# A split matmul's operands: the last chunk's low part made by two DMAs, twelve native chunks a tile instead of 38

## The chip, the cores and the metric

The kernel runs on one core of one Trainium2 chip. The metric is the device time of one execution in microseconds (us), lower is better. Engines are named as in the profile: PE is TensorE (its matmuls), PEld its weight loads, DVE is VectorE, ACT is ScalarE, POOL is GpSimd, SP is SyncE, which here only issues DMAs. A name with a q behind it (SPq, POOLq) is the queue in which that engine issues.

## The reference

A batch of 1024 samples looks up 33 rows of 128 numbers, one in each of 33 tables. From each sample's 33 rows the 528 products of all pairs are formed, sent through a small dense layer, scored against the sample's feature vector and averaged with a softmax over the pairs. A three-layer network ends it.

```python
row, col = np.triu_indices(33, k=1)
inner = x[:, row] * x[:, col]                                   # 1024 x 528 x 128
fm = relu(einsum('bpd,ad->bpa', inner, attn_W) + attn_b)        # the large matmul
scores = einsum('ba,bpa->bp', gnn_feature, fm)
attn = softmax(scores, axis=1)
attn_output = einsum('bp,bpd->bd', attn, inner) * 100.0
h = concatenate([gnn_feature, attn_output, gnn_feature], axis=1)
h = relu(h @ W_top1 + b_top1); h = relu(h @ W_top2 + b_top2); y = h @ W_top3
```

All of it is in 32-bit floating point.

## The kernel before, in words

The batch is cut into 8 tiles of 128 samples, a tile into 32 steps of 4 samples; S counts the 256 steps of the kernel, s those of a tile. One step has 4 x 528 = 2112 columns (pairs of samples and field pairs), cut into five chunks of 416 or 424 columns; two chunks fill one slot of the ring of output banks.

**One step** passes through the engines so. DVE forms the products of the pairs, 128 x 2112, into `inner` (`product`, L413). The dense layer then can be done in two ways, chunk by chunk. A **native** chunk is one matmul in 32-bit (L577), which the profile shows as two instructions. A **split** chunk takes three matmuls on operands of the type fp32r: ACT rounds the products to it (`round_inner`, L310, into `inner_hi`), DVE subtracts the rounded part from the products (`rest_of_inner`, L420, into `inner_lo`), and PE adds up low weights times high part, high weights times low part, and high times high (L584, L585, L586). The list `NATIVE` says how many chunks at the front of each step are native: one in most steps, two in six steps of a tile, four and three in the very first two. So a tile has 38 native chunks of its 160. The rounding and the subtraction run over the rest of the step in one instruction each.

ACT takes two chunks at a time out of the output banks (`relu`, L302, into `fm`). Five such pairs of chunks make up two steps; j = 0 and 1 come in the even step, 2 to 4 in the odd one. After each even step but the first PE multiplies the `fm` of the two steps before it with blocks of the feature vectors (`reduce_steps`, L607), which gives the scores.

**Beside the steps** other work of the neighbouring tiles is placed at fixed steps s by lists: at 7, 10, 13 and 16 PE multiplies the softmax weights of the tile before with its looked-up rows (`fields`, L631), and DVE weighs and sums the result one step later (L470, L478). At 18, 20, 22, 24 and 26 PE turns the looked-up rows of the next tile (`transpose_x`, L617), and ACT copies them out (L341) and repeats some of them (L331). At 19, 21 and 23 the final network of the tile before runs (`mlp`, L641 to L656; ACT L349 to L355). At the start of a tile come the row maximum (DVE L434), the exponentials (ACT L317), their scaling (ACT L326) and a transposition (DVE L450). All units that need an output bank share a ring of three banks in a fixed order.

**Queues.** Each engine's program is written out by hand in the order of the steps. In the iteration S, ACT does the first relu of S, the rounding of S + 2, then the other relus; DVE does the low part of S + 1, the weighing, and the product of S + 3. POOL only gathers: 33 indirect DMAs a tile (`gather`, L274), one after another, as soon as the rows of the tile before were turned. SP stores a tile's rows in DRAM (`store_rows`, L224), loads them again with fields and samples exchanged (`load_fields`, L213), and spreads the transposed softmax weights (`spread_attn`, L218); its order goes by tiles, with a wait ahead of each item.

**Buffers.** `inner` and `inner_hi` have three buffers, `inner_lo` two, `fm` three. The product of S waits for the low part and the native chunks of S - 3, the rounding of S for all chunks of S - 3, the low part of S for all chunks of S - 2. PE waits for a step's low part at its first split chunk.

Of the kernel before, what the change touches and what calls it, by code (L numbers as in the profile page):

```python
# [7 lines left out]
ALU = mybir.AluOpType  # L8
# [4 lines left out]
def afm_tower(nc, gnn, ids, tables, w1, b1, w2, b2, w3, attn_w, attn_b, out):  # L13
# [47 lines left out]
    LAST_FIELDS_AT = (ALL - 3, ALL - 2)  # L61

# [22 lines left out]
    with ctx:  # L85
# [12 lines left out]
        inner = sb("inner", [D, INNER_BUFS, COLS])  # L98
        inner_hi = sb("inner_hi", [D, HI_BUFS, SPLIT], FP32R)
        inner_lo = sb("inner_lo", [D, LO_BUFS, SPLIT], FP32R)  # L100
# [11 lines left out]
        w3_sb = sb("w3_sb", [P, M2])  # L112
        b1_sb = sb("b1_sb", [P, M1])
        b2_sb = sb("b2_sb", [P, M2])
        attn_wt = sb("attn_wt", [D, P])
        attn_wt_hi = sb("attn_wt_hi", [D, P], FP32R)
        attn_wt_lo = sb("attn_wt_lo", [D, P], FP32R)
        attn_b_sb = sb("attn_b_sb", [P, 1])
        gnn_t = sb("gnn_t", [P, B])
        pooled = sb("pooled", [D, P])  # L120
        h1 = sb("h1", [P, M1, P])
        h2 = sb("h2", [P, M2, P])
        y_row = sb("y_row", [1, P])
        ident = sb("ident", [P, P])
        neg_max = sb("neg_max", [P, 1])
        exp_sum = sb("exp_sum", [P, 1])
        inv_sum = sb("inv_sum", [P, 1])


        gnn_rows = x_fields[:, 0, 0:T, :]  # L130
        attn_w_rows = x_fields[:, 1, 0, :]
        weighted = attn[:].rearrange("p a b -> p (a b)").rearrange("p (b f) -> p b f", f=I)
        weighted_tail = inner[:, 0, 0:QS * FN * I].rearrange("p (b f) -> p b f", f=I)
# [20 lines left out]
        s_lo = sem("inner_lo_ready")  # L154
        s_hidden = sem("hidden_ready")
# [39 lines left out]

        def native_cols(S):
            return EDGES[S % 2][NATIVE[S]]

# [9 lines left out]
        def _(sp):  # L208
# [11 lines left out]

            def store_rows(t):
# [15 lines left out]
            store_rows(1)  # L237
# [4 lines left out]
            for t in range(T - 1):  # L242
                sp.wait_ge(s_inv, 3 * (t + 1))
                spread_attn(0)
                spread_attn(1)
                for c in (2, 3):
                    sp.wait_ge(s_fields_done, FJ * t + c - 1)
                    load_fields(t, c, x_fields[:, c % 2], s_fields[c % 2])
                    spread_attn(c)
                if t + 2 < T:  # L250
                    store_rows(t + 2)
# [15 lines left out]
        def _(pool):  # L267
# [17 lines left out]
            for t in range(T):  # L285
                gather(t)
# [113 lines left out]
        def _(dve):  # L400
# [126 lines left out]
            for S in range(ALL):  # L527
                t, s = divmod(S, STEPS)
                if S + 1 < ALL:
                    rest_of_inner(S + 1)  # L530
# [188 lines left out]
```

## Time and profile before

| What | us |
|---|---|
| Median of three runs (lowest, highest) | 1272.69 (1272.43, 1273.11) |
| The profiled execution's own time | 1272.05 |
| Its span, from the first to the last instruction | 1269.9 |
| PE busy in the span | 1203.5 |
| PE's weight loads busy | 898.6 |
| DVE busy | 1153.3 |
| ACT busy | 1018.9 |
| POOL busy | 465.4 |
| Moved by DMA | 58.87 MB |

The profile is of one execution. A busy time is the time in which at least one instruction of the engine ran; PE's matmuls are pipelined and overlap in the profile, so what one costs is read from the distance between the starts of two, not from its own duration. DVE and ACT instructions that follow each other without a wait overlap by some 0.1 us too. Starts and windows are counted from the span's start. "x" stands ahead of a count, a shape is partitions x elements, and the text after "<-" in square brackets or behind the last bar is what ended the idle time before the instruction.

### The profile page before, as it was taken

How to read it: one execution, taken by the hardware profiler on the slowest of the kernel's cores; microseconds unless marked ns; L12 is line 12 of the kernel's file. 1: busy time of each engine (PE TensorE's matmuls, PEld its weight loads, DVE VectorE, ACT ScalarE, POOL GpSimd, SP SyncE). 2: the span in 40 equal slices, each digit the busy share in tenths (PEclk: the TensorE clock that was granted, in tenths of full speed). 3: DMA queues.
4: the chain of work that ended last, by engine and by line, in shares of the span. 5: the costliest groups of instructions: out<-in, count | busy, mean ns of one | idle time of the engine just before them, and what ended most of it. 6: DMA issues, size and time to landing. Idle time of an engine off the chain costs nothing.

```text
span 1269.9 us, 21243 instructions
## 1 busy us (share of the span) xinstructions
PE 1203.5 (95%) x8732; PEld 898.6 (71%) x8732; DVE 1153.3 (91%) x649; ACT 1018.9 (80%) x1039; POOL 465.4 (37%) x270
## 2 busy tenths in 40 slices
PE   1499999999999999999999999999999999999998
PEld 1277777777777777777777777777777777777766
DVE  2399899998999989999899989999899998999994
ACT  1288898778987889878897798977888788887783
POOL 6586684018810388005850078201880000000000
PEclk9999999999999999999999999999999999999999
DMA  4212311311103111131101301031110300011001
GB/s 108 99 34 82 72 30 28 111 36 28 32 17 127 28 28 33 30 106 36 30 22 48 105 26 34 20 110 39 30 32 20 121 18 1 1 29 39 18 9 38
DMA packets 54863, 58.87 MB, mean 46 GB/s; under 512 B 10728, under 2 KB 49136, under 8 KB 53744
## 3 DMA queue, kind: packets, MB, share of 16 engines
q1 hardware_dynamic: 46304, 40.20, 10.5%
q0 software_dynamic: 8448, 17.32, 5.2%
q8 instruction: 69, 1.13, 0.4%
q14 instruction: 26, 0.21, 0.1%
q10 hardware_dynamic: 16, 0.00, 0.0%
HBM read 36.12 MB, written 17.31 MB: 42 GB/s over the span
## 4 chain that ended last, share of the span: by engine, by line
PE 77%; ACT 8%; issue 7%; DVE 6%; POOL 2%; DMA 0%; DVEq 0%; ACTq 0%; POOLq 0%
PE scores L607 18%; PE ring L577 16%; PE ring L584 12%; PE ring L585 11%; PE ring L586 11%; ACT fm L302 3%; PE ring L631 3%; DVE inner L413 3%; ACT inner_hi L310 3%; POOL x_rows L274 2%; PE ring L617 2%; DVE inner_lo L420 2%; PE ring L651 1%; ACT exp_pairs L317 1%; DVE attn L470 1%
## 5 line engine op out<-in xcount | busy, mean ns | idle before, releaser
L302 ACT ACTIVATE fm<-ring,attn_b_sb 128x848 f32<-128x848 f32 (+1 forms) x640 | 597.1, 971 | 184.9 <-PE ring L577 176.8
L413 DVE TENSOR_TENSOR inner<-xt 128x2112 f32<-128x2112 f32 x256 | 602.6, 2354 | 66.9 <-ACT xt L341 37.0
L274 POOL DMA_INDIRECT x_rows<-in_tbl,ids_all x264 | 464.7, 1760 | 489.0 <-PE ring L617 399.3
L420 DVE TENSOR_TENSOR inner_lo<-inner,inner_hi 128x1688 fp32r<-128x1688 f32 (+4 forms) x256 | 466.9, 1824 | 24.5 <-ACT inner_hi L310 21.6
L584 PE MATMUL ring<-inner_hi,attn_wt_lo 128*128 128x424 f32 (+1 forms) x971 | 434.4, 447 | 5.1 <-ACT fm L302 4.4
L310 ACT CAST inner_hi<-inner 128x1688 fp32r<-128x1688 f32 (+4 forms) x256 | 392.3, 1532 | 5.3 <-DVE inner L413 5.3
L585 PE MATMUL ring<-inner_lo,attn_wt_hi 128*128 128x424 f32 (+1 forms) x971 | 344.1, 354 | 0.0
L586 PE MATMUL ring<-inner_hi,attn_wt_hi 128*128 128x424 f32 (+1 forms) x971 | 344.0, 354 | 0.0
L577 PE MATMUL ring<-inner,attn_wt 128*128 128x424 f32 (+1 forms) x618 | 276.5, 543 | 10.2 <-issue 6.5
L607 PE MATMUL scores<-fm,gnn_blocks 128*32 128x264 f32 x4096 | 254.6, 389 | 6.3 <-ACT exp_pairs L317 6.3
L584 PEld LDWEIGHTS ring<-inner_hi,attn_wt_lo 128*128 128x128 f32 x971 | 182.8, 188 | 73.2 <-issue 39.0
L585 PEld LDWEIGHTS ring<-inner_lo,attn_wt_hi 128*128 128x128 f32 x971 | 183.2, 189 | 43.4 <-issue 40.3
L607 PEld LDWEIGHTS scores<-fm,gnn_blocks 128*32 128x32 f32 x4096 | 119.9, 109 | 108.0 <-issue 13.3
L586 PEld LDWEIGHTS ring<-inner_hi,attn_wt_hi 128*128 128x128 f32 x971 | 182.4, 188 | 5.3
L577 PEld LDWEIGHTS ring<-inner,attn_wt 128*128 128x128 f32 x618 | 104.8, 190 | 85.5 <-issue 76.9
L617 PE MATMUL ring<-ident,x_rows 128*128 128x128 f32 x264 | 39.2, 293 | 34.0 <-DMA x_rows<-in_tbl,ids_all 31.1
L631 PE MATMUL ring<-attn_t,x_fields 128*128 128x128 f32 x512 | 62.5, 275 | 1.4 <-ACT attn_t L395 1.4
L341 ACT COPY xt<-ring 128x1024 f32<-128x1024 f32 (+1 forms) x40 | 38.5, 966 | 31.3 <-PE ring L617 19.6
L631 PEld LDWEIGHTS ring<-attn_t,x_fields 128*128 128x128 f32 x512 | 61.9, 191 | 2.4 <-issue 2.2
L617 PEld LDWEIGHTS ring<-ident,x_rows 128*128 128x128 f32 x264 | 33.0, 151 | 39.5 <-DMA x_rows<-in_tbl,ids_all 25.1
L470 DVE TENSOR_TENSOR attn<-ring,xt 128x1024 f32<-128x1024 f32 x30 | 36.6, 1219 | 2.1 <-PE ring L631 2.1
L478 DVE TENSOR_REDUCE pooled<-attn 128x32 f32<-128x1024 f32 x30 | 36.4, 1214 | 0.1
(53 smaller groups left out, 204.7 us busy)
## 6 DMA issues: line engine op xcount, KB each, us to landing
x_dram<-x_rows SPq DMA_DIRECT2D x8, 2112.0 KB, 6.6
x_fields<-x_dram SPq DMA_DIRECT2D x128, 128.0 KB, 3.0
x_rows<-in_tbl,ids_all POOLq DMA_INDIRECT x264
attn_t<-attn_turned SPq DMA_DIRECT2D x124, 32.0 KB, 1.9
w_sb<-in_W_top SPq DMA_DIRECT2D x2, 512.0 KB
x_fields<-in_r_gnn_feature SPq DMA_DIRECT2D x1, 512.0 KB, 4.2
h<-in_W_top SPq DMA_DIRECT2D x1, 256.0 KB
ids_all<-in_ids SPq DMA_DIRECT2D x1, 132.0 KB, 2.8
```

The costliest lines, as they stand in the source:

```text
L274: nc.gpsimd.indirect_dma_start(out=x_rows[:, f, :], out_offset=None, in_=tables[f], in_offset=bass.IndirectOffsetOnAxis(ap=ids_all[:, t, f ...
L302: nc.scalar.activation(dst, slot(("hidden", pair, j))[:, :, 0:n], ACT.Relu, bias=attn_b_sb[:, 0:1]).then_inc(s_fm, 1)
L310: nc.scalar.copy(inner_hi[:, S % HI_BUFS, 0:COLS - at], inner[:, S % INNER_BUFS, at:]).then_inc(s_hi, 1)
L413: nc.vector.tensor_tensor(dst, a, b, ALU.mult).then_inc(s_inner, 1)
L420: nc.vector.tensor_tensor(inner_lo[:, S % LO_BUFS, 0:COLS - at], inner[:, S % INNER_BUFS, at:], inner_hi[:, S % HI_BUFS, 0:COLS - at].bitc ...
L577: nc.tensor.matmul(dst, attn_wt[:], inner[:, S % INNER_BUFS, begin:end], start=True, stop=True)\
L584: nc.tensor.matmul(dst, attn_wt_lo[:], hi, start=True, stop=False)
L585: nc.tensor.matmul(dst, attn_wt_hi[:], lo, start=False, stop=False)
L586: nc.tensor.matmul(dst, attn_wt_hi[:], hi, start=False, stop=True).then_inc(s_hidden, 1)
L607: last = nc.tensor.matmul(scores[I * j:I * j + I, h, 0:HALF], block_of(s, j), fm[:, S % FM_BUFS, at:at + HALF], start=s == 0, stop=s == ST ...
L617: last = nc.tensor.transpose(to[:, n // 4, n % 4 * P:(n % 4 + 1) * P], x_rows[:, FU * c + n, :], ident[:])
L631: last = nc.tensor.matmul(bank[:, h, to:to + QS * I], x[:, n, :], own[:, :, n, :], start=True, stop=True)
```

## The change

It does these things:

- **Native chunks.** Twelve steps of a tile (s = 2, 3, 5, 6, 9, 10, 12, 13, 15, 16, 18, 19) have one native chunk, the other twenty none. The kernel's first two steps are native as a whole.
- **Low part of the last chunk by DMA.** In every step from the third on, the fifth chunk's low part isn't made by DVE. SP copies the chunk's products, once they are there, into a buffer of their own (`inner_lo_dma`, three buffers); POOL then issues a DMA that adds the rounded part onto it. PE waits for that DMA ahead of the last chunk's matmuls.
- **Sign.** ACT rounds the products with a factor of -1, so that the DMA can add and DVE too; the low and the high weights that meet the negative high part are negated at the start.
- **In place.** DVE writes the other chunks' low part over the products themselves (the same memory under a second name). `inner` has four buffers, `inner_lo` is gone, and the product of S waits for all chunks of S - 4.
- **Order of SP and POOL.** Both now go by steps. SP, in iteration S: the spreading of the first two weights at s = 5, the copy for step S + 3, loads of fields and spreading one step after PE's `fields`, the store of the next tile's rows at s = 18. POOL, in iteration S: the add for step S + 2, then one or two gathers, from s = 27 of one tile to s = 16 of the next.
- **Memory.** Some small tensors (`h1`, `h2`, `y_row`, biases, softmax scalars) lie in spare parts of others; ACT's scaling of the softmax weights waits for the stored output of the tile before because of it.

The diff, cut to its core:

```diff
-    NATIVE_2 = (2, 5, 8, 11, 14, 17)
-    NATIVE = [2 if S % STEPS in NATIVE_2 else 1 for S in range(ALL)]
-    NATIVE[0], NATIVE[1] = 4, 3
-    SPLIT = COLS - THIN
-    INNER_BUFS, HI_BUFS, LO_BUFS, FM_BUFS = 3, 3, 2, 3
+    NATIVE_1 = (2, 3, 5, 6, 9, 10, 12, 13, 15, 16, 18, 19)
+    NATIVE = [1 if S % STEPS in NATIVE_1 else 0 for S in range(ALL)]
+    FIRST = 2
+    for S in range(FIRST):
+        NATIVE[S] = CHUNKS
+    LAST = CHUNKS - 1
+    INNER_BUFS, HI_BUFS, FM_BUFS = 4, 3, 3
+    DMA_BUFS, STORE_AT, SPREAD_AT = 3, 18, 5
...
+    def gathers_of(S):
+        t, s = divmod(S + 5, STEPS)
+        return t + 1, [f for f in range(F) if f * 2 // 3 == s] if t + 1 < T else []
...
+            def copy_last(S):
+                sp.wait_ge(s_inner, S + 1)
+                if S >= FIRST + DMA_BUFS:
+                    sp.wait_ge(s_hidden, CHUNKS * (S - DMA_BUFS + 1))
+                begin, end = EDGES[S % 2][LAST], EDGES[S % 2][LAST + 1]
+                sp.dma_start(inner_lo_dma[:, S % DMA_BUFS, 0:end - begin].bitcast(FP32),
+                             plain[:, S % INNER_BUFS, begin:end]).then_inc(s_copied[S % DMA_BUFS], 16)
...
+            def take_off_hi(S):
+                pool.wait_ge(s_hi, split_steps(S))
+                at, begin, end = native_cols(S), EDGES[S % 2][LAST], EDGES[S % 2][LAST + 1]
+                pool.wait_ge(s_copied[S % DMA_BUFS], dma_turn(S))
+                nc.gpsimd.dma_start(inner_lo_dma[:, S % DMA_BUFS, 0:end - begin].bitcast(FP32),
+                                    inner_hi[:, S % HI_BUFS, begin - at:end - at].bitcast(FP32), accum_op=ALU.add)\
+                    .then_inc(s_added[S % DMA_BUFS], 16)
...
-            for t in range(T):
-                gather(t)
+            for f in range(F):
+                gather(0, f)
+            for S in range(-5, ALL):
+                if 0 <= S and S + 2 < ALL:
+                    take_off_hi(S + 2)
+                t, some = gathers_of(S)
+                for f in some:
+                    gather(t, f)
...
-                nc.scalar.copy(inner_hi[:, S % HI_BUFS, 0:COLS - at], inner[:, S % INNER_BUFS, at:]).then_inc(s_hi, 1)
+                nc.scalar.activation(inner_hi[:, S % HI_BUFS, 0:COLS - at], plain[:, S % INNER_BUFS, at:], ACT.Copy, scale=-1.0)\
+                    .then_inc(s_hi, 1)
...
                 if S >= INNER_BUFS:
-                    dve.wait_ge(s_lo, S - INNER_BUFS + 1)
-                    dve.wait_ge(s_hidden, CHUNKS * (S - INNER_BUFS) + NATIVE[S - INNER_BUFS])
+                    dve.wait_ge(s_hidden, CHUNKS * (S - INNER_BUFS + 1))
...
             def rest_of_inner(S):
-                dve.wait_ge(s_hi, S + 1)
-                if S >= LO_BUFS:
-                    dve.wait_ge(s_hidden, CHUNKS * (S - LO_BUFS + 1))
-                at = native_cols(S)
-                nc.vector.tensor_tensor(inner_lo[:, S % LO_BUFS, 0:COLS - at], inner[:, S % INNER_BUFS, at:],
-                                        inner_hi[:, S % HI_BUFS, 0:COLS - at].bitcast(FP32), ALU.subtract).then_inc(s_lo, 1)
+                dve.wait_ge(s_hi, split_steps(S))
+                at, end = native_cols(S), EDGES[S % 2][LAST]
+                nc.vector.tensor_tensor(inner[:, S % INNER_BUFS, at:end], plain[:, S % INNER_BUFS, at:end],
+                                        inner_hi[:, S % HI_BUFS, 0:end - at].bitcast(FP32), ALU.add).then_inc(s_lo, 1)
...
                     if c == NATIVE[S]:
-                        pe.wait_ge(s_lo, S + 1)
+                        pe.wait_ge(s_lo, split_steps(S))
+                    if c == LAST:
+                        pe.wait_ge(s_added[S % DMA_BUFS], dma_turn(S))
```

SP's new order, in place of its loop over the tiles:

```python
copy_last(FIRST)
for S in range(ALL):
    t, s = divmod(S, STEPS)
    part = part_at(S, SPREAD_AT)
    if part == T - 1:
        part = None
    if S == ALL - FN + TURN_AT:
        part = T - 1
    if part is not None:
        sp.wait_ge(s_inv, 3 * (part + 1))
        spread_attn(0)
        spread_attn(1)
    if S + 3 < ALL:
        copy_last(S + 3)
    for c in range(FJ):
        if s == FIELDS_AT[c] + 1 and t > 0:
            sp.wait_ge(s_fields_done, FJ * (t - 1) + c + 1)
            if c < 2:
                load_fields(t - 1, c + 2, x_fields[:, c % 2], s_fields[c % 2])
                spread_attn(c + 2)
            else:
                sp.wait_ge(s_store, 16 * (t + 1))
                load_fields(t, c - 2, x_fields[:, c % 2], s_fields[c % 2])
    if s == STORE_AT and t + 1 < T:
        store_rows(t + 1)
```

## Rows read from the trace of the kernel before

**Rows 1.** The page, part 1: busy time, share of the span, instructions.

```profile
PE 1203.5 (95%) x8732; PEld 898.6 (71%) x8732; DVE 1153.3 (91%) x649; ACT 1018.9 (80%) x1039; POOL 465.4 (37%) x270
```

**Rows 2.** The page, part 4: the chain that ended last, by engine.

```profile
PE 77%; ACT 8%; issue 7%; DVE 6%; POOL 2%; DMA 0%; DVEq 0%; ACTq 0%; POOLq 0%
```

**Rows 3.** Busy time by window: length, then PE, PEld, DVE, ACT, POOL.

```profile
502.80:574.90 72.10, 70.73 (x526) 52.40 (x524) 71.56 (x44) 57.63 (x58) 3.51 (x2) 1.00 0.20 64
574.90:623.20 48.30, 47.56 (x340) 36.65 (x336) 41.71 (x23) 42.94 (x47) 35.45 (x18) 1.00 0.12 32
623.20:653.20 30.00, 30.00 (x229) 21.88 (x228) 29.66 (x15) 26.36 (x26) 25.46 (x15) 1.00 0.13 34
```

**Rows 4.** Timeline of PE from 478.2: start, duration, engine, line, operation.

```profile
478.20 0.87 PE L577 MATMUL ring<-inner,attn_wt 128*128 128x424 f32 x2
...
479.11 0.36 PE L585 MATMUL ring<-inner_lo,attn_wt_hi 128*128 128x424 f32 x1
...
479.69 0.35 PE L585 MATMUL ring<-inner_lo,attn_wt_hi 128*128 128x424 f32 x1
...
486.36 0.87 PE L577 MATMUL ring<-inner,attn_wt 128*128 128x424 f32 x2
```

**Rows 5.** Timeline of DVE, two places.

```profile
478.47 1.93 DVE L420 TENSOR_TENSOR inner_lo<-inner,inner_hi 128x1696 fp32r<-128x1696 f32 x1
...
482.59 1.91 DVE L420 TENSOR_TENSOR inner_lo<-inner,inner_hi 128x1688 fp32r<-128x1688 f32 x1
...
526.89 1.46 DVE L420 TENSOR_TENSOR inner_lo<-inner,inner_hi 128x1264 fp32r<-128x1264 f32 x1
```

**Rows 6.** Timeline of ACT, two places.

```profile
480.85 1.61 ACT L310 CAST inner_hi<-inner 128x1688 fp32r<-128x1688 f32 x1
...
497.37 1.26 ACT L310 CAST inner_hi<-inner 128x1264 fp32r<-128x1264 f32 x1
...
585.11 0.96 ACT L302 ACTIVATE fm<-ring,attn_b_sb 128x832 f32<-128x832 f32 x1 [0.81 <-PE ring L577]
...
596.48 0.96 ACT L302 ACTIVATE fm<-ring,attn_b_sb 128x832 f32<-128x832 f32 x1 [0.72 <-PE ring L577]
```

**Rows 7.** The page, part 5: busy time and mean ns of one; idle before.

```profile
L302 ACT ACTIVATE fm<-ring,attn_b_sb 128x848 f32<-128x848 f32 (+1 forms) x640 | 597.1, 971 | 184.9 <-PE ring L577 176.8
...
L585 PE MATMUL ring<-inner_lo,attn_wt_hi 128*128 128x424 f32 (+1 forms) x971 | 344.1, 354 | 0.0
```

**Rows 8.** Timeline of SP: a set of loads, a set of spreads.

```profile
544.43 1.79 SPq L213 DMA_DIRECT2D x_fields<-x_dram  x4
546.26 2.41 SPq L218 DMA_DIRECT2D attn_t<-attn_turned  x4
```

**Rows 9.** The page, part 6: DMAs, KB each, us from issue to landing.

```profile
x_dram<-x_rows SPq DMA_DIRECT2D x8, 2112.0 KB, 6.6
...
attn_t<-attn_turned SPq DMA_DIRECT2D x124, 32.0 KB, 1.9
```

**Rows 10.** Timeline of POOL: one gather at the start, two in the steps.

```profile
13.44 0.95 POOL L274 DMA_INDIRECT x_rows<-in_tbl,ids_all  x1 [0.30 <-issue]
...
489.77 1.96 POOL L274 DMA_INDIRECT x_rows<-in_tbl,ids_all  x1 [0.30 <-issue]
492.04 1.53 POOL L274 DMA_INDIRECT x_rows<-in_tbl,ids_all  x1 [0.31 <-issue]
```

**Rows 11.** Timeline of PE at the start: what waits for the eighth gather.

```profile
16.11 1.94 PE L617 MATMUL ring<-ident,x_rows 128*128 128x128 f32 x8 [7.16 <-DMA x_rows<-in_tbl,ids_all]
```

**Rows 12.** Timeline of DVE beside the two gathers.

```profile
490.83 1.91 DVE L420 TENSOR_TENSOR inner_lo<-inner,inner_hi 128x1688 fp32r<-128x1688 f32 x1
492.66 2.35 DVE L413 TENSOR_TENSOR inner<-xt 128x2112 f32<-128x2112 f32 x1
```

More of the change, by code:

```diff
@@ L97, in afm_tower @@
         xt = sb("xt", [D, 2, P, FX])
-        inner = sb("inner", [D, INNER_BUFS, COLS])
+        plain = sb("products", [D, INNER_BUFS, COLS])
+        inner = nc.alloc_sbuf_tensor_at("low_parts", [D, INNER_BUFS, COLS], FP32R, offset=nc.sbuf_base - INNER_BUFS * COLS * 4)
+        inner_lo_dma = sb("inner_lo_dma", [D, DMA_BUFS, WIDE], FP32R)
         inner_hi = sb("inner_hi", [D, HI_BUFS, SPLIT], FP32R)
-        inner_lo = sb("inner_lo", [D, LO_BUFS, SPLIT], FP32R)
         fm = sb("fm", [P, FM_BUFS, COLS])
@@ L154, in afm_tower @@
         s_lo = sem("inner_lo_ready")
+        s_copied = [sem(f"last_chunk_copied{i}") for i in range(DMA_BUFS)]
+        s_added = [sem(f"last_chunk_hi_taken_off{i}") for i in range(DMA_BUFS)]
+        s_wt_neg = sem("negative_weights_ready")
         s_hidden = sem("hidden_ready")
@@ L194, in fields_in, with split_steps, dma_turn @@
             return min(FU, F - FU * c)
+        def split_steps(S):
+            return S - FIRST + 1
+        def dma_turn(S):
+            return 16 * len(range(S, FIRST - 1, -DMA_BUFS))
         def native_cols(S):
@@ L267, in _, with gather @@
         def _(pool):
[L268 to L277 removed]
+            def gather(t, f):
+                c = f // FU
+                if t > 0:
+                    pool.wait_ge(s_xt_done, XJ * (t - 1) + c + 1)
+                    pool.wait_ge(s_store, 16 * t)
+                nc.gpsimd.indirect_dma_start(
+                    out=x_rows[:, f, :], out_offset=None, in_=tables[f],
+                    in_offset=bass.IndirectOffsetOnAxis(ap=ids_all[:, t, f:f + 1], axis=0),
+                ).then_inc(s_gather[c], 16)
+            def take_off_hi(S):
[5 more added lines that the diff above has]
+                    .then_inc(s_added[S % DMA_BUFS], 16)
             nc.gpsimd.memset(ident[:], 1.0).then_inc(s_const, 1)
@@ L576, in hidden @@
                     if c < NATIVE[S]:
-                        nc.tensor.matmul(dst, attn_wt[:], inner[:, S % INNER_BUFS, begin:end], start=True, stop=True)\
+                        nc.tensor.matmul(dst, attn_wt[:], plain[:, S % INNER_BUFS, begin:end], start=True, stop=True)\
                             .then_inc(s_hidden, 1)
@@ L670, in _ @@
             pe.wait_ge(s_setup, 6)
+            pe.wait_ge(s_wt_neg, 1)
             pe.wait_ge(s_weights, 96)
```

81 lines of the change are left out of this document (30 added, 51 removed).

## The prediction

> **What bounds the kernel now.** I read the busy line first: in a span of 1269.9 us TensorE is busy 95%, VectorE 91%, ScalarE 80% and GpSimd 37% [rows 1]. The chain that ended last is 77% TensorE, 8% ScalarE, 6% VectorE and 7% issue [rows 2]. So TensorE sets the end nearly everywhere, with two engines close behind, and the question is what each has to spare in each stretch. I cut one tile (32 steps, 150.4 us, from 502.8 to 653.2) at TensorE's steps [rows 3]. Stretch A, steps 2 to 16 (softmax, weighted fields): 72.10 us, PE 70.73, DVE 71.56, ACT 57.63: VectorE has no gap. Stretch B, steps 17 to 26 (x_t and MLP): 48.30 us, PE 47.56, DVE 41.71, ACT 42.94: TensorE. Stretch C, steps 27 to 31, 0 and 1: 30.00 us, PE 30.00, DVE 29.66, ACT 26.36: two engines full. Eight such tiles are 1203 us; 67 us are start and end.
>
> **Prices.** TensorE: a native chunk starts at 478.20 and the second product of the next split chunk at 479.11; less that chunk's first product (0.19) it is 0.72 us. The split chunk between second products is 479.69 - 479.11 = 0.58 [rows 4]. So a chunk turned from native to split gives TensorE 0.14 us back. VectorE: a low part of 1696 columns takes 1.92 and one of 1264 takes 1.46, 0.45 per chunk of some 424; a whole step (low part, product) takes 482.59 - 478.47 = 4.12 [rows 5]. ScalarE: the cast takes 1.61 for 1688 columns and 1.26 for 1264, 0.35 a chunk [rows 6].
>
> **The change, counted per tile.** Native chunks 38 to 12: 26 more split chunks. TensorE -26 x 0.14 = -3.6 us. ScalarE now rounds every split chunk, +26 x 0.35 = +9.1 us. VectorE takes off 26 more but leaves 32 last chunks to the DMAs: -6 x 0.45 = -2.7 us. In the whole kernel: 309 native chunks become 96 + 10 (steps 0 and 1 are all native now), TensorE -203 x 0.14 = -28 us, ScalarE +71, VectorE -23 (971 low chunks [rows 7] become 1174 less 254 last ones).
>
> By stretch, from where the native steps lie:
> A: native chunks 20 to 10, so PE -1.4 and ACT +3.5; low chunks 55 to 50, DVE -2.2. Busy: PE 69.3, DVE 69.3, ACT 61.1. PE now stands 1.4 over its busy time, DVE 0.5. With both margins kept A becomes 70.7 or 69.8: gain 1.4 to 2.3; I take 1.6, nearer PE's, whose waits (softmax, ring slots) stay.
> B: native 11 to 2, PE -1.3; ACT 42.94 + 9 x 0.35 = 46.1, DVE 41.3. The sum would allow 1.3, but the load is uneven: between two first relus of odd steps, 585.11 and 596.48, ScalarE idles only 0.72 of 11.37 us [rows 6] and gets 2 x 0.35 more, so that pair gains nothing. There are two such pairs of the five; the rest gain up to 0.29 each. Gain 0.8.
> C: native 7 to 0, PE -1.0 to 29.0, ACT 28.8, DVE unchanged at 29.66, which is the new bound. Gain 0.3.
> Sum 2.7 us a tile, 8 x 2.7 = 21.6.
>
> Edits that cost nothing or little. The sign: casts become scaled activations. The nearest row is the relu, 971 ns for mostly 848 columns [rows 7], where the cast's rate gives 1.26 - 0.35 = 0.91; so between 0 and 0.06 more each, at most 15 us of ScalarE, hidden but in B; I take 0. The product waits for the whole of step S-4 instead of the native chunk of S-3, which is a little earlier on TensorE: worth 0 to 0.7 us of freedom where DVE idles, none on the path. The first wait for the low part now stands ahead of chunk 0 in native-0 steps. The low part that follows the cast of 480.85 starts at 482.59 [rows 5, 6], ends at 484.5, and its step starts at 486.36 [rows 4]; with a cast 0.35 longer 1.5 us stay spare: 0, with the relu and the cast as cover. Steps 0 and 1: 3 more native chunks, +0.4, but two casts and low parts less ahead of them: 0. The scaled attention's added wait is for an output stored at least four steps earlier. Set-up on ScalarE lies under the first gathers: 0. PE, ACT and DVE keep the places of their other jobs.
>
> SP issues 254 copies more, at 0.45 us each by the fields' loads (4 in 1.79 us) [rows 8]. Its queue is now ordered by steps: the eight spreads at step 5 (0.60 each, 4.8 us) and loads with spreads at steps 8 and 11 (4.2 us) stand ahead of the next copy, which is at most some 0.7 us late; it has over 1 us. A 2112 KB store takes 6.6 us to land [rows 9] ahead of the copy of step 22 in the same queue, issued a step (4.6 us) later: some 2 us late, still ahead of its cast. Cost 0, cover gone if a copy needs over 4 us.
>
> **The new chain to the last chunk**, which no row of before shows: cast, accumulating DMA on POOL, last chunk. Take the even step that starts at T = 478.20. The cast for two steps on ends at 480.85 + 1.61 = T + 4.26, T + 4.6 with its fifth chunk; the last chunk of that step starts at T + 8.16 + 4 x 0.58 = T + 10.5 [rows 4, 6]. POOL needs 0.94 for a gather of 64 KB with VectorE idle, and TensorE starts 1.72 us after such a gather's end [rows 10, 11]. More bytes: (6.6 - 1.9) us over 2080 KB from the store and the spread [rows 9], 0.35 us for 153 KB more, twice as much for read and add: the add lands 0.94 + 1.72 + 0.7 = 3.4 us after the cast, T + 8.0. Spare 2.5 us. Low bound of the cost 0, high bound below. I charge 1.5 us in all for steps with two gathers.
>
> POOL is the resource to watch. Gathers are now strewn over steps 27 to 31 and 0 to 16, 33 in 22 steps, with an add in each. Beside VectorE a gather takes 1.53 and 1.96 in turn: both end 0.9 us after a VectorE instruction starts (490.83 to 491.73 and 492.66 to 493.57), so a gather waits for a border between two [rows 10, 12]; two of them with 2 x 0.30 fill a step, 2.05 each. The add costs POOL 0.94 + 0.30 = 1.24 if it doesn't wait so, 2.05 if it does. Then 33 x 2.05 + 22 x 1.24 = 95 us, or 113, for steps that would last 102.1 - 1.9 = 100.2 us. I take 1.24, since the waiting fits the read of the indices, which the add doesn't have.
>
> Two pages pull apart here. The Trainium skill (GPSIMD Engine Reference, Key points) says that GpSimd shares its SBUF interfaces with VectorE and contends with every VectorE instruction of two SBUF inputs; taken at its word the add waits as the gathers do, 113 us, which is rival 3 below. The Trainium skill (SBUF — State Buffer, SBUF: two separate sides) narrows this to GpSimd instructions that read SBUF; by that the add, which only writes its transfer list, gives 95 us. The trace shows the waiting of the gathers (0.94 alone, 1.53 and 1.96 beside VectorE), which both allow, and nothing that tells the two apart.
>
> **Sum.** Against the profiled execution's 1272.05 (span 1269.9 and 2.15 around it): 1272.05 - 21.6 + 1.5 = 1252; the median stands 0.6 above it: 1252.6, forecast 1253.
>
> **The rivals.**
> 1. TensorE alone decides, since a fourth product buffer lets VectorE run ahead: 1272.7 - 28 = 1244. For it: PE's 77% of the chain. Against: DVE full in A and C.
> 2. ScalarE takes it. Its 9.1 us a tile come into 23.5 us of idle time, much of it waits for chunk 0 of an odd step, which aren't free time. If B gets longer by 1.5 us instead of shorter by 0.8 and A gives 1.2 only, the gain is 0 a tile: 1264 to 1275.
> 3. Slower: POOL gets late in the 22 steps. It decides where an add costs POOL over (100.2 - 67.7)/22 = 1.48 us. At 2.05 the stretch lasts 113 us, 12.6 more on each of seven tiles, 1341; at 1.75, 1295; VectorE's short instructions in A give more borders, so 1275 to 1340, with 1297 the middle. The same happens without POOL if the add takes over 5.9 us from cast to landing: TensorE then waits at the last chunk, and relus, casts and products behind it shift too. For it: 2.5 transfers a step where two fill it. Against: the add has no index to read.
> The swap of native for split chunks is plain in the diff; that it doesn't happen is no case.
>
> **How the numbers follow.** The forecast 0.55 (1244 to 1262); rival 1 0.05 (to 1244); rival 2 0.15 (half faster by over 0.2%, most of the rest within); rival 3 0.25. About 0.2% (2.5 us) is what a measurement can tell here. Faster 0.55 + 0.05 + 0.07 = 0.67; same 0.06 + 0.01 = 0.07; slower 0.26. The range runs from 1243 to 1300: it leaves out 0.05 below and 0.12 above. The forecast's own range is 1244 to 1262.
>
> **What would show it.** TensorE's busy time near 1175, ScalarE near 1090, VectorE near 1130. In a tile's windows A near 70.5, B near 47.5, C near 29.7. The add's own duration on POOL at 0.9 to 1.0, and no wait of the last chunk for the add's DMA beyond 2 us in all. Wrong if the waits show TensorE waiting for the DMA into the low part, if POOL is over 90% busy in the 22 steps, or if ScalarE's cast leads the chain over B and C.

## The result and the profile after

The changed kernel takes 1316.10 us (median of 5 runs, 1310.14 to 1319.13), the kernel before 1272.43 on the same chip. The ratio is 1.0333, with a 95% interval from 1.032 to 1.0345: slower, where 1253 was forecast, and outside the range. The times are spread over 9 us, those of before over 1.

The page of the changed kernel: busy time, the chain by engine, and groups (line, engine, operation, count | busy us, mean ns | idle before it).

```profile
PE 1199.7 (92%) x8935; PEld 934.7 (71%) x8935; DVE 1130.8 (86%) x647; ACT 1088.2 (83%) x1038; POOL 689.6 (53%) x524
...
PE 59%; ACT 16%; issue 12%; DVE 5%; DMA 3%; POOL 3%; SPq 1%; another core or an unknown queue 1%; POOLq 0%; ACTq 0%; DVEq 0%
...
L351 ACT ACTIVATE fm<-ring,exp_pairs 128x848 f32<-128x848 f32 (+1 forms) x640 | 595.1, 968 | 159.5 <-PE ring L636 99.5
L634 PE MATMUL ring<-inner_hi,attn_wt_lo_neg 128*128 128x424 f32 (+1 forms) x1174 | 473.9, 404 | 49.5 <-DMA inner_lo_dma<-inner_hi 24.0
L309 POOL DMA_INDIRECT x_rows<-in_tbl,ids_all x264 | 455.6, 1726 | 91.3 <-issue 77.8
L318 POOL DMA_DIRECT2D inner_lo_dma<-inner_hi x254 | 237.4, 935 | 498.3 <-ACT inner_hi L359 448.3
L359 ACT ACTIVATE inner_hi<-products 128x1688 fp32r<-128x1688 f32 (+1 forms) x254 | 466.4, 1836 | 0.3 <-DVE products L462 0.3
```

VectorE (1130.8) and ScalarE (1088.2) are where the forecast put them (1130, 1090), TensorE is at 1199.7 in place of 1175. TensorE's part of the chain fell from 77% [rows 2] to 59%; ScalarE, "issue" and DMA took it. An add costs GpSimd 935 ns. The idle time ahead of L634 is new: 24.0 us for the DMA into the low part.

I cut the span at the row maxima, one a tile. The first three before (L434) and after (L481), start and duration:

```profile
202.22 0.70 DVE L434 TENSOR_REDUCE neg_max<-scores 128x1 f32<-128x528 f32 x1
352.68 0.70 DVE L434 TENSOR_REDUCE neg_max<-scores 128x1 f32<-128x528 f32 x1
```

```profile
212.45 0.70 DVE L481 TENSOR_REDUCE exp_pairs<-scores 128x1 f32<-128x528 f32 x1
363.86 0.70 DVE L481 TENSOR_REDUCE exp_pairs<-scores 128x1 f32<-128x528 f32 x1
514.92 0.70 DVE L481 TENSOR_REDUCE exp_pairs<-scores 128x1 f32<-128x528 f32 x1
```

Before, all six distances are 150.3 to 150.5 us. After, they are 151.4, 151.1, 161.2, 154.0, 161.0 and 151.1. So the span's 38.4 us more (1308.3 less 1269.9) have three parts: the **start** 10.2 (212.45 - 202.22); **three long tiles** 10.1, 2.9 and 9.9 over the quiet ones, 22.9; and six times nearly 0.8 for **quiet tiles**, 4.6, which had been forecast 2.7 shorter each. The tail adds 0.7.

A quiet tile in the stretches of [rows 3], same columns:

```profile
363.70:435.96 72.26, 69.94 (x537) 54.01 (x536) 70.74 (x45) 61.52 (x58) 56.96 (x40) 1.00 0.64 147
435.96:484.40 48.44, 47.26 (x349) 38.06 (x345) 39.62 (x22) 45.46 (x47) 10.80 (x11) 1.00 0.55 143
484.40:514.80 30.40, 29.72 (x235) 22.97 (x235) 29.78 (x15) 28.79 (x26) 22.26 (x15) 1.00 0.46 111
```

TensorE is busy less than before in each, and none of the three is shorter. In C no engine is full any more.

**The long tile.** GpSimd, VectorE and TensorE in the tile of 161.2 us:

```profile
531.84 13.55 POOL L309 DMA_INDIRECT x_rows<-in_tbl,ids_all  x1 [0.30 <-issue]
545.33 1.00 POOL L318 DMA_DIRECT2D inner_lo_dma<-inner_hi  x1
```

```profile
532.51 2.36 DVE L462 TENSOR_TENSOR products<-xt 128x2112 f32<-128x2112 f32 x1
534.78 1.93 DVE L467 TENSOR_TENSOR low_parts<-products,inner_hi 128x1688 fp32r<-128x1688 f32 x1
536.60 2.38 DVE L462 TENSOR_TENSOR products<-xt 128x2112 f32<-128x2112 f32 x1
538.86 1.95 DVE L467 TENSOR_TENSOR low_parts<-products,inner_hi 128x1696 fp32r<-128x1696 f32 x1
540.69 2.39 DVE L462 TENSOR_TENSOR products<-xt 128x2112 f32<-128x2112 f32 x1
542.95 1.52 DVE L467 TENSOR_TENSOR low_parts<-products,inner_hi 128x1272 fp32r<-128x1272 f32 x1
```

```profile
548.56 0.72 PE L634 MATMUL ring<-inner_hi,attn_wt_lo_neg 128*128 128x424 f32 x1 [7.30 <-DMA inner_lo_dma<-inner_hi]
```

A gather, in this run 0.94 to 3.3 us but for three, lasts 13.55. VectorE meanwhile goes through six two-input instructions without a gap; the gather ends 0.9 us after the last of them (544.47), when VectorE runs dry. The add behind it starts at once and lands 2.2 us after its end, and TensorE has waited 7.30 us. Behind the wait TensorE's clock is at the lower level for a while (the column after POOL's is the granted clock):

```profile
548.50:556.00 7.50, 7.44 (x32) 7.28 (x33) 2.56 (x2) 2.04 (x3) 5.49 (x6) 0.63 0.58 125
560.00:567.00 7.00, 6.85 (x44) 5.88 (x46) 6.41 (x4) 7.00 (x7) 4.18 (x4) 1.00 0.79 171
```

**The start.** The eight early gathers of tile 1 begin at 54.6, and the first add comes behind them:

```profile
69.89 1.01 POOL L318 DMA_DIRECT2D inner_lo_dma<-inner_hi  x1
```

```profile
73.22 0.68 PE L634 MATMUL ring<-inner_hi,attn_wt_lo_neg 128*128 128x416 f32 x1 [6.41 <-DMA inner_lo_dma<-inner_hi]
```

### The profile page after: what moved, and what is told of

Its sections match the earlier page's. It is cut to its first block, busy times and chain, and to the rows that moved or that the text cites. A ratio compares the mean times of both kernels' runs of the same rounds, so it can differ in the third digit from the quotient of the medians.

```text
span 1308.3 us, 22481 instructions
## 1 busy us (share of the span) xinstructions
PE 1199.7 (92%) x8935; PEld 934.7 (71%) x8935; DVE 1130.8 (86%) x647; ACT 1088.2 (83%) x1038; POOL 689.6 (53%) x524
## 4 chain that ended last, share of the span: by engine, by line
PE 59%; ACT 16%; issue 12%; DVE 5%; DMA 3%; POOL 3%; SPq 1%; another core or an unknown queue 1%; POOLq 0%; ACTq 0%; DVEq 0%
PE scores L657 16%; PE ring L634 12%; PE ring L636 9%; PE ring L635 9%; ACT inner_hi L359 8%; ACT fm L351 6%; PE ring L681 4%; PE ring L623 4%; DVE products L462 3%; POOL x_rows L309 2%; PE ring L667 2%; DMA inner_lo_dma<-inner_hi 2%; DVE low_parts L467 1%; PE ring L701 1%; DMA inner_lo_dma<-products 1%
## 5 line engine op out<-in xcount | busy, mean ns | idle before, releaser
L351 ACT ACTIVATE fm<-ring,exp_pairs 128x848 f32<-128x848 f32 (+1 forms) x640 | 595.1, 968 | 159.5 <-PE ring L636 99.5
L462 DVE TENSOR_TENSOR products<-xt 128x2112 f32<-128x2112 f32 x256 | 601.5, 2351 | 41.4 <-ACT xt L392 37.7
L467 DVE TENSOR_TENSOR low_parts<-products,inner_hi 128x1272 fp32r<-128x1272 f32 (+1 forms) x254 | 445.1, 1752 | 91.5 <-ACT inner_hi L359 87.4
L634 PE MATMUL ring<-inner_hi,attn_wt_lo_neg 128*128 128x424 f32 (+1 forms) x1174 | 473.9, 404 | 49.5 <-DMA inner_lo_dma<-inner_hi 24.0
L318 POOL DMA_DIRECT2D inner_lo_dma<-inner_hi x254 | 237.4, 935 | 498.3 <-ACT inner_hi L359 448.3
L359 ACT ACTIVATE inner_hi<-products 128x1688 fp32r<-128x1688 f32 (+1 forms) x254 | 466.4, 1836 | 0.3 <-DVE products L462 0.3
L636 PE MATMUL ring<-inner_hi,attn_wt_hi_neg 128*128 128x424 f32 (+1 forms) x1174 | 416.5, 355 | 0.0
L635 PE MATMUL ring<-low_parts,attn_wt_hi 128*128 128x424 f32 (+1 forms) x920 | 326.5, 355 | 0.0
L634 PEld LDWEIGHTS ring<-inner_hi,attn_wt_lo_neg 128*128 128x128 f32 x1174 | 220.9, 188 | 147.0 <-issue 69.9
L636 PEld LDWEIGHTS ring<-inner_hi,attn_wt_hi_neg 128*128 128x128 f32 x1174 | 221.2, 188 | 5.7
```

Of the source, the lines that this page charges most:

```text
L318: nc.gpsimd.dma_start(inner_lo_dma[:, S % DMA_BUFS, 0:end - begin].bitcast(FP32), inner_hi[:, S % HI_BUFS, begin - at:end - at].bitcast(FP ...
L351: nc.scalar.activation(dst, slot(("hidden", pair, j))[:, :, 0:n], ACT.Relu, bias=attn_b_sb[:, 0:1]).then_inc(s_fm, 1)
L359: nc.scalar.activation(inner_hi[:, S % HI_BUFS, 0:COLS - at], plain[:, S % INNER_BUFS, at:], ACT.Copy, scale=-1.0)\
L462: nc.vector.tensor_tensor(dst, a, b, ALU.mult).then_inc(s_inner, 1)
L467: nc.vector.tensor_tensor(inner[:, S % INNER_BUFS, at:end], plain[:, S % INNER_BUFS, at:end], inner_hi[:, S % HI_BUFS, 0:end - at].bitcast ...
L634: nc.tensor.matmul(dst, attn_wt_lo_neg[:], hi, start=True, stop=False)
```

## The experiments

The kernel before ran beside each set: it took 1269.3 us beside most of them, 1272.3 beside the three with both edits, 1269.8 beside the one with the two-column product, and 1272.4 beside the changed kernel. So a run is told by what it takes over the kernel before beside it, ahead of its time; the changed kernel takes 43.7 us over it.

### What takes the gain of a quiet tile

**The add left out:** the plain copy is used as the low part, so the high part isn't taken off the last chunk.

```diff
-                nc.gpsimd.dma_start(inner_lo_dma[...], inner_hi[...], accum_op=ALU.add).then_inc(s_added[S % DMA_BUFS], 16)
...
-                        pe.wait_ge(s_added[S % DMA_BUFS], dma_turn(S))
+                        pe.wait_ge(s_copied[S % DMA_BUFS], dma_turn(S))
```

> The changed kernel without the accumulating DMA: TensorE takes the plain copy of the products for the last chunk's low part (so the high part isn't taken off there), and POOL only waits where it issued the add. The copies by SP stay. Theory A (ScalarE): a quiet tile stays at 151 us, and only the start (8 to 10 us) and the stuck gathers with their half clock (some 23 us in the profiled execution) go: 1278 to 1290. Theory B (the chain of adds holds every tile): a quiet tile falls to 147 or 148 us, and the time to 1250 to 1262.

5.8 over (1275.07 us, ratio 1.0046, 1.0029 to 1.0063). All tiles 151.0 or 151.1, the first row maximum at 200.55, the clock full throughout. The tiles are those of theory A, the time is 3 us under its range. So the add and what stands ahead of it on GpSimd cost the start and the long tiles, 38 us together, and nothing in a quiet tile; and without it there is still no gain. Its gathers get long too, up to 10.07 us, and nobody waits for them:

```profile
L309 POOL DMA_INDIRECT x_rows<-in_tbl,ids_all x264: 942/1524/10067, 4.5 to 1026.7; - x132
```

**Part of ScalarE's cast left out** in steps 20 to 31, 0 and 1: the first chunk's high part isn't made, VectorE and TensorE do all they did.

```diff
+                skip = EDGES[S % 2][1] if S > STEPS // 2 and at == 0 and S % STEPS in (*range(20, 32), 0, 1) else 0
-                nc.scalar.activation(inner_hi[:, S % HI_BUFS, 0:COLS - at], plain[:, S % INNER_BUFS, at:], ACT.Copy, scale=-1.0)\
+                nc.scalar.activation(inner_hi[:, S % HI_BUFS, skip:COLS - at], plain[:, S % INNER_BUFS, at + skip:], ACT.Copy, scale=-1.0)\
```

> The changed kernel with ScalarE's rounding of the first chunk (416 or 424 of 2112 columns) left out in the fourteen steps 20 to 31, 0 and 1 from tile 1 on; VectorE and TensorE do the same instructions as before on the old contents, so the high part of these chunks isn't computed. Theory (in stretches C and the end of B it is ScalarE's 1.96 us rounding between two evacuations of the three-bank ring that keeps TensorE at 8.4 to 8.5 us a pair where its own work is 7.9): these pairs fall to 8.1 to 8.25 us, the seven pairs of a tile give 1.2 to 2 us, quiet tiles are 149 to 150 us in place of 151.1, and the time falls by 8 to 14 us. Rival (VectorE or the DMAs bound these pairs): pairs stay at 8.4 to 8.5 us, quiet tiles at 151.

18.1 over (1287.34 us, 1282.32 to 1296.31). Quiet tiles 149.2, pairs of stretch C 8.08 in place of 8.43, both as the theory has it. The time fell by 25.6, not by 8 to 14: seven tiles at 1.9 each give some 13, the rest lies in the start and the long gathers, which differ from run to run (one over 5 us in this profile). One pair, from scores to scores, by window (length, then PE, PEld, DVE, ACT, POOL busy): before, after, with the short casts.

```profile
489.53:497.74 8.21, 8.21 (x61) 6.06 (x60) 8.21 (x5) 7.38 (x8) 7.00 (x4) 1.00 0.11 32
```

```profile
492.97:501.40 8.43, 8.14 (x63) 6.41 (x63) 8.19 (x5) 8.09 (x8) 7.52 (x6) 1.00 0.46 112
```

```profile
486.99:495.08 8.09, 8.09 (x64) 6.41 (x63) 8.09 (x5) 7.40 (x8) 7.18 (x6) 1.00 0.47 118
```

Before, TensorE and VectorE are full. After, none of the three is: each waits a little for the others, around the ring of three bank pairs. ScalarE empties a slot, casts for 1.98 us, empties the next. What the waits look like in this pair:

```profile
494.43 0.98 ACT L351 ACTIVATE fm<-ring,exp_pairs 128x848 f32<-128x848 f32 x1
495.76 0.96 ACT L351 ACTIVATE fm<-ring,exp_pairs 128x832 f32<-128x832 f32 x1 [0.34 <-PE ring L636]
496.61 1.96 ACT L359 ACTIVATE inner_hi<-products 128x2112 fp32r<-128x2112 f32 x1
498.48 2.67 ACT L351 ACTIVATE fm<-ring,exp_pairs 128x848 f32<-128x848 f32 x3
```

```profile
499.48 0.46 PE L634 MATMUL ring<-inner_hi,attn_wt_lo_neg 128*128 128x424 f32 x1 [0.29 <-ACT fm L351]
```

```profile
494.59 1.93 DVE L467 TENSOR_TENSOR low_parts<-products,inner_hi 128x1696 fp32r<-128x1696 f32 x1 [0.24 <-ACT inner_hi L359]
```

With 0.35 us taken off each cast TensorE and VectorE are full again, at 8.09. The chain followed back through stretch C says the same: the cast has 5.0% of it before, 20.2% in the changed kernel (484.4 to 514.8) and 5.3% with the short casts (480 to 508). The quiet tile is now 1.2 us shorter than before, all of it in B and C, where the forecast had 1.1. The price per chunk was right; that 96% busy is no room was not seen.

**The old count of native chunks** with the new DMAs:

```diff
-    NATIVE = [1 if S % STEPS in NATIVE_1 else 0 for S in range(ALL)]
+    NATIVE = [2 if S % STEPS in (2, 5, 8, 11, 14, 17) else 1 for S in range(ALL)]
```

> The changed kernel with the old number of native chunks (38 a tile), everything else as changed. ScalarE's rounding goes back by 26 chunks x 0.35 = 9.1 us a tile, TensorE gets 3.6 us a tile more. Theory A (ScalarE's extra rounding ate the gain, since ScalarE and TensorE wait for each other around the ring): a tile without a stuck gather takes 149.5 to 150.5 us, slightly less than the 151.1 of the changed kernel, though TensorE has more to do. Theory B (the DMAs' chain costs something in every tile): such a tile takes 153 us or more, TensorE's 3.6 on top. Time by A 1300 to 1316, with the start and the stuck gathers as they are; by B over 1330.

24.9 over (1294.20 us, 1292.38 to 1294.91). Stretch C is back at 8.22 a pair, but the tiles are 150.9 to 153.2, none under those of before, and both theories miss, in the tile and in the time. VectorE is busy 1049.2 us in place of 1153.3 [rows 1], and nothing comes of it: the first row maximum is at 217.36, and TensorE waits for an add 22 times, 26.8 us in all, 9.61 of them at the start.

**The low part of the last chunk by VectorE,** neither copy nor add; the chunk's range in the subtraction becomes `at, end = native_cols(S), COLS`.

> The changed kernel without both DMAs: VectorE makes the whole low part in place, also of the last chunk; native chunks, order of the gathers and buffers stay as changed. VectorE gets 32 x 0.45 = 14.4 us more a tile, 154.5 us of work in all. If VectorE then bounds every tile: 157 to 160 us a tile, 1320 to 1345 in all, no stuck gathers that TensorE waits for. If the time comes out at or below the changed kernel's 1316, the DMAs' relief of VectorE is worth nothing net of what they cost.

49.7 over (1318.99 us, 1317.67 to 1320.15), tiles 157 to 157.9, VectorE busy 1233.2. With few native chunks the DMAs are needed: they are worth 6 us a tile. Gathers are long here in every tile: 20 of the 264 take over 3.3 us, the longest 11.30.

### What makes a gather long

**A memset ahead of each product,** of one column that nothing reads; in the second kernel a product of two columns in its place.

```diff
+                dve.wait_ge(s_gap, S)
+                nc.vector.memset(gap[:], 0.0).then_inc(s_gap, 1)
                 nc.vector.tensor_tensor(dst, a, b, ALU.mult).then_inc(s_inner, 1)
```

```diff
-                nc.vector.memset(gap[:], 0.0).then_inc(s_gap, 1)
+                nc.vector.tensor_tensor(gap[:], attn_wt[:, 0:1], attn_wt[:, 1:2], ALU.mult).then_inc(s_gap, 1)
```

> The changed kernel with one small VectorE memset (one column, no operand to read) ahead of each product, so that GpSimd finds in every step a moment in which VectorE holds no instruction with two SBUF inputs. Theory (a gather on GpSimd starts only in such a moment, and back to back low part, product, low part leave none it can take when VectorE is behind): no gather longer than 3.3 us where the changed kernel had 13.55, 8.04 and 9.90 us, no half clock after the start, tile periods all within 151 to 153 us (the three long ones were 161.2, 154.0 and 161.0), and 1316 falls by 15 to 25 us to 1291 to 1301; the start stays 10 us late. Rival (a gather waits for VectorE's queue to run empty, or for its own descriptors, and not for a kind of instruction): gathers of 8 to 14 us stay and the time is 1310 to 1325, 32 memsets a tile of about 0.06 us adding at most 2 us a tile.

> The changed kernel with a small instruction ahead of each product as in the run with the memset (1290.6 us, no gather over 3.3 us), but the small instruction is now a product of two columns in SBUF, so that VectorE gets the same count of instructions and semaphore steps and no moment free of two-input work. Theory (what a gather on GpSimd needs is a moment without a two-input instruction of VectorE): the long gathers come back, two or more over 7 us in the profiled execution, a first row maximum at 210 to 214 us, and a time of 1300 to 1325 us with a spread over 5 us. Rival (any further instruction, or the wait ahead of it, breaks VectorE's sequence enough): no gather over 3.3 us, 1288 to 1294 us and a spread of about 1 us, as with the memset.

With the memset 21.3 over (1290.6 us, 1289.93 to 1290.79): 22 us less by 256 further instructions, and the spread falls from 9 us to 0.9. With the two-column product 34.8 over (1304.52, 1293.32 to 1315.32), two tiles of 161. The gathers' least, median and longest ns, first with the memset, then with the product:

```profile
L311 POOL DMA_INDIRECT x_rows<-in_tbl,ids_all x264: 941/1399/3210, 4.6 to 1043.3; - x132
```

```profile
L311 POOL DMA_INDIRECT x_rows<-in_tbl,ids_all x264: 940/1324/13879, 4.4 to 1062.5; - x132
```

Both came out as the first theory of each expectation has it, but for one execution of the second at 1293.32, and the memset's time lies 0.4 us under its range. The same place in both, VectorE and GpSimd, with the memset:

```profile
532.60 0.06 DVE L465 MEMSET exp_pairs<- 128x1 f32 x1
```

```profile
531.86 1.72 POOL L311 DMA_INDIRECT x_rows<-in_tbl,ids_all  x1 [0.30 <-issue]
```

and with the product of two columns:

```profile
534.55 0.19 DVE L465 TENSOR_TENSOR exp_pairs<-attn_wt 128x1 f32<-128x1 f32 x1
```

```profile
533.79 13.88 POOL L311 DMA_INDIRECT x_rows<-in_tbl,ids_all  x1 [0.31 <-issue]
```

The gather beside the memset ends 1.0 us after the memset starts. A moment without a two-input instruction of VectorE lets a gather through, and one more two-input instruction does not; count and semaphore steps are the same in both kernels. The memset took away the long tiles, and the spread with them.

Such a moment is enough, but it isn't the only way through. The second long gather of the changed kernel ends 1.0 us after a low part starts, at a border of two two-input instructions without a gap:

```profile
693.10 8.04 POOL L309 DMA_INDIRECT x_rows<-in_tbl,ids_all  x1 [0.30 <-issue]
```

```profile
697.87 2.33 DVE L462 TENSOR_TENSOR products<-xt 128x2112 f32<-128x2112 f32 x1
700.13 1.90 DVE L467 TENSOR_TENSOR low_parts<-products,inner_hi 128x1696 fp32r<-128x1696 f32 x1
```

It had missed three such borders by then. Two gathers without the add (10.07 and 7.79 us) and one with the gathers at steps 20 to 4 (7.74) end the same way. In the kernel before, gathers take such borders too [rows 10, 12], and none of its 264 is over 3.13 us. Which border a gather gets and which it misses isn't shown; that a VectorE far behind, with its next instruction ready, makes it miss is only argued. The run in which VectorE makes the whole low part fits that, with long gathers in every tile.

**The gathers at steps 20 to 4,** two a step, those of tile 1 at 0 to 16:

```diff
-        t, s = divmod(S + 5, STEPS)
-        return t + 1, [f for f in range(F) if f * 2 // 3 == s] if t + 1 < T else []
+        t, s = divmod(S + 12, STEPS) if S >= STEPS - 12 else (0, S)
+        return t + 1, [f for f in range(F) if f // 2 == s] if t + 1 < T else []
```

> The changed kernel with the gathers of a tile at steps 20 to 4, two a step (about where the kernel before had them), in place of steps 27 to 16; those of tile 1 at steps 0 to 16. Nothing else is moved. Theory (a long gather needs VectorE behind, as it is in steps 4 to 19, where its work fills 70.7 of 72.3 us; in steps 20 to 4 it waits for its inputs and leaves a gap at the first change of instruction): no gather over 3.3 us from tile 1 on, row maxima 151 to 152.5 us apart, the first at 200 to 204 us, time 1275 to 1287. Rival (two gathers at 1.5 us and an add of 0.94 us are too much for GpSimd in a step of 4.2 us, so that the add comes late in each): TensorE waits over 1 us for the added part in ten or more steps a tile, row maxima 154 to 160 us apart, time 1295 to 1330.

42.8 over (1312.10 us, 1297.59 to 1331.32), a miss for both: four gathers over 3.3 us stay, one at the start. Of the three in the tiles two are over 7 us (7.74 and 11.86), and both begin some 15 us behind a row maximum, near step 4, where stretch A has begun and the last gathers of a tile still ran. Fewer gathers in A are enough for long ones.

```profile
996.42 11.86 POOL L309 DMA_INDIRECT x_rows<-in_tbl,ids_all  x1 [0.30 <-issue]
```

### What makes the start late

**The first two adds ahead of their turn,** behind three and six of the early gathers:

```diff
+                if S in (-3, -1):
+                    take_off_hi(FIRST if S == -3 else FIRST + 1)
-                if 0 <= S and S + 2 < ALL:
+                if 2 <= S and S + 2 < ALL:
                     take_off_hi(S + 2)
```

> The changed kernel with one edit: POOL issues the adds of steps 2 and 3 after three and six of the eight early gathers of tile 1, not behind all eight. In the trace of the changed kernel the first add is issued at 69.9 us and TensorE waits 6.4 us for it, and the clock is at half for 6.8 us around it. Theory 1 (a start cost of its own): the wait goes, the first row maximum comes 7 to 10 us earlier than at 212.5, and the time falls by 7 to 10 us, to 1302 to 1310. Rival (the start is bound by something else, such as the gathers' rows): less than 3 us.

32.9 over (1302.17 us, 1294.17 to 1318.09), the first row maximum at 213.68: no gain at the start. TensorE's one wait of 6.41 us became three, of 2.44, 1.25 and 5.46. So it isn't the place of the first two adds among the gathers. The profiled execution is faster (1294.17) for another reason: no gather in it is over 4.42 us.

**Tile 1's gathers from step 0,** its store at step 23; then the same with the memset.

```diff
         t, s = divmod(S + 5, STEPS)
+        if t == 0:
+            s = S
...
-                if s == STORE_AT and t + 1 < T:
+                if s == (STORE_AT if t > 0 else 23) and t + 1 < T:
```

> The changed kernel with the gathers of tile 1 begun at step 0 (three in two steps, as in the later tiles) in place of eight of them ahead of the first add, and tile 1's rows stored at step 23 in place of 18. Theory (the start lost 10.2 us because GpSimd works off those eight gathers first, TensorE waits 6.4 us for the first add and runs at half clock for 6.8 us): the first row maximum comes at 200 to 203 us of the span where it was 212.45, TensorE waits under 1 us for the adds of steps 2 and 3, and the time falls by 8 to 12 us to 1304 to 1308. Rival (the start is overloaded on GpSimd whatever the order: moving the first adds ahead of the gathers left 9.1 us of waits): row maximum after 209, gain under 3 us. A later long gather can still hide the gain in a single execution; the row maximum tells.

> The changed kernel with both earlier edits: the one column memset ahead of each product, and the gathers of tile 1 begun at step 0. Theory (the start was lost to gathers that stand ahead of the first adds; with the later start alone a gather of 7.73 us at 63.07, while VectorE went back to back through products and low parts, took the saving away): with a moment free of two-input work in each step no gather at the start is over 3.3 us, the first row maximum comes at 200 to 203 us, TensorE waits under 2 us for adds there, and the time is that of the first edit alone (1290.6) less 9 to 12: 1279 to 1283. Rival (GpSimd is overloaded at the start, with 1.5 gathers and an add in each step): row maximum after 208 and over 1286 us.

Alone 43.6 over (1312.86 us, 1308.45 to 1326.64), first row maximum 208.71: less than half of what was expected, and a long gather appears right there. Its tiles have three more, the longest 14.38 us. With the memset 8.1 over (1280.39, 1280.20 to 1282.78), first row maximum 204.11; TensorE waits for no add at the start.

```profile
63.07 7.73 POOL L311 DMA_INDIRECT x_rows<-in_tbl,ids_all  x1 [0.30 <-issue]
```

```profile
63.69 2.69 POOL L313 DMA_INDIRECT x_rows<-in_tbl,ids_all  x1 [0.30 <-issue]
```

The start needs both edits. With the memset alone the first row maximum stays at 212.33, and TensorE waits 9.48 us for the first add; the eight gathers ahead of that add took 0.95 to 2.54 us, none of them long. With the later gathers alone it is 208.71, with both 204.11. So eight gathers ahead of the first add cost most of the start, and once they are moved a long gather takes over half of it back. The rest, 204.1 against 202.2, isn't explained; it was outside the expected 200 to 203.

### Can it beat the kernel before

Both edits again, with 24 and with 27 native chunks a tile.

```diff
-    NATIVE = [1 if S % STEPS in NATIVE_1 else 0 for S in range(ALL)]
+    NATIVE = [2 if S % STEPS == 5 else 0 if S % STEPS in (0, 4, 14, 20, 22, 24, 26, 28, 30) else 1 for S in range(ALL)]
```

```diff
-    NATIVE = [1 if S % STEPS in NATIVE_1 else 0 for S in range(ALL)]
+    NATIVE = [0 if S % STEPS in (4, 7, 8, 11, 14) else 1 for S in range(ALL)]
```

> As the run with both edits, and 24 native chunks a tile in place of 12: 2 at step 5, none at steps 0, 4, 14, 20, 22, 24, 26, 28 and 30, one elsewhere, so that in steps 20 to 1 every second cast is 0.35 us shorter. Theory (the ring cycle of ScalarE and TensorE sets these pairs: 8.43 us with two full casts, 8.22 with two short ones and 0.28 more of TensorE's work): these pairs come to 8.1 to 8.3 us, quiet tiles to 149.3 to 150.5 us in place of 151.1, and the time falls by 5 to 12 us below that of both edits alone, to 1268 to 1277. Rival (TensorE's longer native chunks cost as much as the casts give): quiet tiles 150.8 to 151.5, within 3 us of both edits alone.

> As the run with both edits, with 27 native chunks a tile: none at steps 4, 7, 8, 11 and 14, one elsewhere. Theory (as for 24, with all casts of steps 15 to 3 short): pairs of steps 20 to 1 as in the kernel before (8.2 to 8.4 us), quiet tiles 149.8 to 150.8 us, time 1270 to 1280. Rival (TensorE's native chunks cost what the casts give): quiet tiles 151 or more, time as of both edits alone or above.

24 chunks: 1270.99 us (10 runs, 1269.36 to 1273.77) against 1272.32, ratio 0.9989 (0.9979 to 0.9999): 0.1% under the kernel before, less than this kernel's measurement can tell for sure. 27 chunks: 1275.01, ratio 1.0017 (1.0007 to 1.0027). Both times and the best tiles, 149.2 and 150.2 us, are within or next to what the theories gave. In the first, pairs of stretch C take 8.22 as before and those of B 11.37, 10.86 and 10.27, the last two 0.10 and 0.16 less than before; the pair of steps 19 and 20 still varies from 11.36 to 12.59 between tiles, and why is open.

## Why the prediction was wrong

**The prices held,** but for TensorE's. "0.94 + 0.30 = 1.24": an add measured 0.935. "1.72 + 0.7": it landed 2.2 us after GpSimd's end, forecast 2.4. ScalarE's and VectorE's busy time came within 2 us. TensorE's came 25 us over the forecast (16 in the run without the add, 1190.8); five split chunks on end still stand 0.58 us apart, and what the rest consists of wasn't taken apart.

**The step that failed first is "By stretch".** A "gain 1.4 to 2.3; I take 1.6", B "Gain 0.8", C "Gain 0.3" were worked out from each engine's busy time alone, stretch by stretch. Measured: A 0.2 us longer, B 0.1, C 0.4. In C "DVE unchanged at 29.66, which is the new bound" was right only when ScalarE had 0.35 us less a cast (8.09 a pair). At 28.8 of 30 us ScalarE isn't full, but its cast stands between two evacuations of the ring, and TensorE can't go on without them. The forecast saw just that for two pairs of B and didn't ask it of C. Rival 2 ("the gain is 0 a tile: 1264 to 1275") is nearly what the run without the add shows (1.0046 of 1272.7 is 1278.6, a little above it). The largest part of the miss is A, 1.8 of 3.4 us a tile, and its cause stays open. There the two pairs of steps that kept their two native chunks got 0.43 us longer (9, 10: 9.91 to 10.34; 15, 16: 9.92 to 10.35), and two that lost three and two got 0.6 shorter (7, 8: 10.32 to 9.69; 13, 14: 10.43 to 9.81). So a pair's time there doesn't follow its own native chunks. The pair 3, 4 went from 8.94 to 9.30 and is back at 8.94 with 24 chunks, with the same native chunks as in the changed kernel; what differs is step 5, whose cast and low part are made during that pair and are a chunk shorter. No run cut ScalarE's casts alone there, so whether the cast or the low part does it isn't shown.

**The second is "I charge 1.5 us in all for steps with two gathers"** with nothing for the start, where only "Steps 0 and 1" were priced, at 0, and the first adds behind eight gathers weren't. The gathers' duration came from two rows in which each took the next border [rows 10, 12], and was applied to stretch A, where VectorE has no gap [rows 3] and where before the change hardly a gather ran (two in 72 us). There one gather missed six borders. The charge was 1.5 us; the long tiles cost 22.9 and the start 10.2. Rival 3 named the place and the outcome (TensorE late for the add, 1275 to 1340 with 1297 the middle), but its mechanism, the add at over 1.48 us of GpSimd, didn't happen: adds took 0.94 and didn't wait; gathers did, and the add stood in their queue. That the time lies within its range bears out its place, not its sum. In the tiles the cost isn't spread over 22 steps but falls on two or three gathers in a profile.

On the two pages weighed: the Trainium skill (SBUF — State Buffer, SBUF: two separate sides) held for the add, which took 0.94 us beside VectorE, and the broader key point of the GPSIMD Engine Reference didn't. The same section of the Trainium skill says that whichever of the two starts first keeps the port pair for its whole instruction and the other is blocked that long. Here the gather of 13.55 us stayed blocked over six instructions, and ended 0.9 us after the last.

**Of the signs named,** TensorE's wait for the DMA into the low part (24.0 us, 2 at most allowed) and the windows (72.3, 48.4 and 30.4 against 70.5, 47.5 and 29.7) spoke clearly. GpSimd over 90% busy did not occur (56.96 of 72.26 us in A, 22.26 of 30.40 in C). The cast didn't lead the chain over B and C either (12.2% of it, TensorE's `scores` 20.6%), though it had 4.0% before; so this sign was set too high for what ScalarE did.

## What to carry to other kernels

Where three engines hand one ring of buffers round, an engine under full isn't one with room: before work is moved there, add up the cycle and look at what stands between two of its steps on the same engine. Before something urgent is put on a queue, look at the longest, not the mean, of what stands ahead of it, and measure that in the stretch where it will run. A spread of the times far over the kernel's usual one is worth a look by itself: here one instruction of 59 ns a step took it away, and 22 us with it.

## What the runs showed of the hardware

A gather issued by GpSimd (index in SBUF) could stay unfinished while VectorE ran products and low parts with two SBUF inputs back to back, for up to 14.38 us, though a new one began every 1.4 to 2.3 us; others got through at such a border, 1.53 and 1.96 us long in the kernel before [rows 10]. With a memset of 59 ns ahead of each product none of 264 took over 3.21 us; with a tiny instruction of two SBUF inputs in its place two took 13.8 and 13.9. A direct accumulating DMA from SBUF to SBUF, issued by the same engine, never took over 1.08 us, and landed 212 KB 2.2 us after that. After a wait of 7.30 us TensorE's granted clock was lower (0.63 over the 7.5 us from there, so mostly the lower of its two levels, 1.2 GHz), and was 1.00 again by 560; the tile with waits of 1.87 and 0.45 us kept the full clock and was 2.9 us longer, the one with 7.30 was 10.1 longer.
